# Moving projected blocks, norm steps and rows of maxima between the slots of VectorE's order

## What is computed

```python
x = x + 0.5 * ffn(layernorm(x))
x = x + attn(layernorm(x))
x = x + 0.5 * ffn(layernorm(x))
```

## Time and profile before

| | us |
|---|---|
| median of 3 runs | 2292.26 |
| lowest and highest | 2292.16, 2292.42 |
| the profiled execution's own time | 2292.54 |
| its span in the trace | 2290.7 |

### The profile page before, as it was taken

One profiled execution on the slowest core, in us unless ns is written; L12 is line 12 of the kernel. 1 busy time (PEld: TensorE's weight loads), 2 busy tenths in 40 slices (PEclk: granted clock), 3 DMA queues, 4 the chain that ended last, 5 costly groups with the idle time before them and its releaser, 6 DMA issues.

```text
span 2290.7 us, 47462 instructions
## 1 busy us (share of the span) xinstructions
PE 2220.2 (97%) x18960; PEld 1480.6 (65%) x18960; DVE 1578.8 (69%) x3138; ACT 1204.1 (53%) x1933; POOL 1064.0 (46%) x864
## 2 busy tenths in 40 slices
PE   2999999999999999999999999999999999999998
PEld 2888875555565565565555555555555655688887
DVE  7766589887777877777877876777777753454543
ACT  4433331566656666566566566666656666533332
POOL 1866653443443443443434434333433434465655
PEclk9999999999999999999999999999999999999999
DMA  5211121111111110110211111010110110011110
GB/s 216 81 42 34 39 58 30 22 41 31 35 32 40 34 51 24 33 40 22 50 42 31 32 35 32 20 42 16 26 42 11 24 36 19 26 29 36 28 39 19
DMA packets 157957, 88.26 MB, mean 39 GB/s; under 512 B 103588, under 2 KB 149924, under 8 KB 156968
## 3 DMA queue, kind: packets, MB, share of 16 engines
q1 hardware_dynamic: 157592, 85.19, 14.0%
q10 hardware_dynamic: 144, 0.03, 0.0%
HBM read 62.87 MB, written 11.80 MB: 33 GB/s over the span
## 4 chain that ended last, share of the span: by engine, by line
PE 90%; DVE 7%; issue 1%; POOL 1%; DMA 0%; ACT 0%; SPq 0%; POOLq 0%; DVEq 0%; ACTq 0%
PE PS L1193 42%; PE PS L1211 21%; PE PS L1223 11%; PE PS L1256 11%; DVE arena L968 2%; PE PS L1235 1%; PE PS L1175 1%; PE PS L1297 1%; PE PS L1283 1%; DVE XN L848 1%; DVE arena L945 1%; DVE turned L931 0%; DVE arena L930 0%; DVE parts L1044 0%; DVE arena L953 0%
## 5 line engine op out<-in xcount | busy, mean ns | idle before, releaser
L1193 PE MATMUL PS<-XT,WGU 128*128 128x256 f16 x9216 | 1115.1, 273 | 37.1 <-DVE WGU L814 20.8
L1193 PEld LDWEIGHTS PS<-XT,WGU 128*128 128x128 f16 x9216 | 876.7, 98 | 264.5 <-issue 135.4
L600 POOL TENSOR_TENSOR arena<-arena 128x512 f16<-128x512 f32 x384 | 451.1, 1175 | 1116.0 <-ACT arena L679 1115.9
L968 DVE TENSOR_REDUCE arena<-PS 128x1 f32<-128x512 f32 x1024 | 657.6, 684 | 327.4 <-PE PS L1223 325.0
L702 ACT ACTIVATE arena<-PS,fac 128x512 f32<-128x512 f32 x1024 | 647.2, 684 | 242.3 <-PE PS L1235 241.1
L672 ACT ACTIVATE arena<-PS,fac 128x512 f32<-128x512 f32 x384 | 263.9, 687 | 753.3 <-PE PS L1193 753.3
L1211 PE MATMUL PS<-WD,arena 128*128 128x256 f16 x4608 | 568.1, 273 | 7.1 <-DVE X L960 4.7
L1211 PEld LDWEIGHTS PS<-WD,arena 128*128 128x128 f16 x4608 | 431.1, 98 | 151.9 <-issue 93.6
L595 POOL TENSOR_TENSOR arena<-arena 128x512 f32<-128x512 f32 x384 | 501.2, 1305 | 46.0 <-DVE arena L953 37.5
L945 DVE SCALAR_TENSOR_TENSOR arena<-arena,PS 128x512 f32<-128x512 f32 x384 | 261.1, 680 | 263.3 <-ACT arena L672 262.4
L1223 PE MATMUL PS<-arena 48*128 48x512 f16 x1024 | 312.5, 382 | 3.3 <-DVE arena L968 2.4
(11 more groups left out here) (116 smaller groups left out, 725.9 us busy)
## 6 DMA issues: line engine op xcount, KB each, us to landing
arena<-ce_scratch SPq DMA_DIRECT2D x256, 128.0 KB, 3.2
arena<-wgu SPq DMA_DIRECT2D x4, 1536.0 KB, 12.9
arena<-q_scratch SPq DMA_DIRECT2D x192, 32.0 KB
arena<-ktab_c SPq DMA_DIRECT2D x16, 256.0 KB, 3.9
q_scratch<-arena SPq DMA_DIRECT2D x32, 128.0 KB, 1.9
out<-X SPq DMA_DIRECT2D x8, 512.0 KB, 2.9
X<-wd SPq DMA_DIRECT2D x2, 1536.0 KB, 22.8
X<-x SPq DMA_DIRECT2D x1, 3072.0 KB, 11.6
```

The costliest lines, as they stand in the source:

```text
L600: pool.tensor_tensor(hs[1][:, d % HS, :], tw[d % 2], hs[0][:, d % HS, :], ALU.subtract).then_inc(lo_done, 1)
L968: dve.tensor_reduce(mx[:, half * REP * QT + c:half * REP * QT + c + 1], PS[:, B_MAX + half, :], AX_X, ALU.max).then_inc(max_taken, 1)
L1193: ins = pe.matmul(PS[:, b, j * HALF_G:(j + 1) * HALF_G], WGU[w][:, kt, part * CHUNKS + c + j, :], XT[r][:, k % 2, kt, half * HALF_G:(half ...
```

## The change

It changes no arithmetic and no instruction, only the places. `join_slots` gives 8, 10, 14 for k = 1 and 2 and 10, 14, 16 for k = 3 to 8 (so no block in slot 12), with `rope_sum`, `rope_high`, `rope_low` and `store_block` following their block by one to three slots. In k = 1 to 8 the norm steps of group k+1 go to s = 6, 7, 9, 11, POOL's inverse roots to 8, `rows_high` and `rows_low` to 12, and SP's `turn_group` to slot 13. In the other groups these stay. On DVE `max_rows` leaves the visit: it comes behind `product` for position 0, ahead of the third visit for position 1 or behind the event, where there is no third visit, and behind the event for position 2. The loads of units wait two slots more where they use block 2.

```diff
--- before.py
+++ after.py
@@ -110,7 +110,7 @@
 
 
 
-P_HI, P_LO, P_JOIN, T_HI, T_LO, T_LOGITS = 6, 7, 8, 15, 16, 17
+P_HI, P_LO, T_HI, T_LO, T_LOGITS = 6, 7, 15, 16, 17
 
 
 BY_PE, JOINS_BY_PE = (0, 3), (0, 1)
@@ -118,9 +118,19 @@
 KV_ROWS = K_ROWS + KV * HD
 
 
-def join_slot(g):
-
-    return P_JOIN if g in JOINS_BY_PE else P_JOIN + 2
+
+NORM_AT, ALONE_AT = ((6, 7, 9, 11), 8, 12), ((9, 10, 11, 12), 10, 13)
+
+
+def steps_of_norm(k):
+
+    return NORM_AT if 1 <= k <= GROUPS else ALONE_AT
+
+
+
+def join_slots(k):
+
+    return () if k not in range(1, GROUPS + 1) else (8, 10, 14) if k - 1 in JOINS_BY_PE else (10, 14, 16)
 
 
 def event_table():
@@ -131,8 +141,8 @@
             if k - 1 in JOINS_BY_PE:
                 at[k * PER_GROUP + P_HI].append(("p_hi", k - 1, 0))
                 at[k * PER_GROUP + P_LO].append(("p_lo", k - 1, 0))
-            for j in range(JOINS):
-                at[k * PER_GROUP + join_slot(k - 1) + 2 * j].append(("join", k - 1, j))
+            for j, s in enumerate(join_slots(k)):
+                at[k * PER_GROUP + s].append(("join", k - 1, j))
         if k + 1 < PREPS:
             for s, name in ((T_HI, "t_hi"), (T_LO, "t_lo"), (T_LOGITS, "logits")):
                 if name == "logits" or k + 1 in BY_PE:
@@ -528,7 +538,7 @@
                     spread((d + 4) // 6)
                 if s == 7 and 1 <= k <= GROUPS and k - 1 not in JOINS_BY_PE:
                     turn_join(k - 1)
-                if s == 14 and 0 <= k < PREPS - 1 and k + 1 not in BY_PE:
+                if s == (13 if 1 <= k <= GROUPS else 14) and 0 <= k < PREPS - 1 and k + 1 not in BY_PE:
                     turn_group(k + 1)
                 if s == 21 and k + 1 < PREPS:
                     write_combine(k + 1)
@@ -536,21 +546,20 @@
                 if 1 <= k <= GROUPS:
                     if s == 1:
                         tables(k - 1)
-                    blk, odd = divmod(s - join_slot(k - 1) - 3, 2)
-                    if blk in range(JOINS) and not odd:
-                        store_block(k - 1, blk)
-                        if not blk:
-                            store_values(k - 1)
+                    if s - 3 in join_slots(k):
+                        store_block(k - 1, join_slots(k).index(s - 3))
+                    if s - 3 == join_slots(k)[0]:
+                        store_values(k - 1)
                 if d == FIRST - 2:
                     load(0)
                     load(1)
-                if d == FIRST:
+                if d == FIRST + 2:
                     load(2)
                 if d == FIRST + 2:
                     for u in range(2):
                         load_values(u)
                 for u in range(UNITS):
-                    if u >= QKV and d == max(SLOT_OF[FILLS * (u - QKV) + FILLS] + 1, 2 * PER_GROUP * (u // KV + 1) + 18):
+                    if u >= QKV and d == max(SLOT_OF[FILLS * (u - QKV) + FILLS] + 1, 2 * PER_GROUP * (u // KV + 1) + 18 + u % KV // 2 * 2):
                         load(u)
                     if u >= 2 and d == max(SLOT_OF[quad_visit(STEPS * (u - 1) - 1)] + 1, FIRST + 3):
                         load_values(u)
@@ -620,9 +629,8 @@
                 k, s = divmod(d, PER_GROUP)
                 if 0 <= d < SLOTS:
                     low(d)
-                blk, odd = divmod(s - join_slot(k - 1) - 2, 2)
-                if 1 <= k <= GROUPS and blk in range(JOINS) and not odd:
-                    rope_low(k - 1, blk)
+                if s - 2 in join_slots(k):
+                    rope_low(k - 1, join_slots(k).index(s - 2))
                 if d + 1 < SLOTS:
                     weigh(d + 1)
                 if 1 <= k <= GROUPS:
@@ -631,9 +639,9 @@
                     if s == 6:
                         rows_low(norm_of_join(k - 1))
                 if 0 <= k < PREPS - 1:
-                    if s == 10:
+                    if s == steps_of_norm(k)[1]:
                         inverse_roots(norm_of_group(k + 1))
-                    if s == 13:
+                    if s == steps_of_norm(k)[2]:
                         rows_low(norm_of_group(k + 1))
                 if d >= 0:
                     for name, n, j in EVENTS[d]:
@@ -764,11 +772,10 @@
                 if 1 <= k <= GROUPS:
                     if s == 6:
                         rows_high(norm_of_join(k - 1))
-                    blk, odd = divmod(s - join_slot(k - 1) - 2, 2)
-                    if blk in range(JOINS) and not odd:
-                        rope_high(k - 1, blk)
+                    if s - 2 in join_slots(k):
+                        rope_high(k - 1, join_slots(k).index(s - 2))
                 if 0 <= k < PREPS - 1:
-                    if s == 13:
+                    if s == steps_of_norm(k)[2]:
                         rows_high(norm_of_group(k + 1))
                     if s == T_LOGITS + 1:
                         exponentials(k + 1)
@@ -985,8 +992,13 @@
                 f = v + AHEAD
                 if f < VISITS:
                     maximum(f)
-                    if f % FILLS == FILLS - 1:
-                        max_rows(f // FILLS)
+
+
+            def unit_ends(v):
+
+                f = v + AHEAD
+                if f < VISITS and f % FILLS == FILLS - 1:
+                    max_rows(f // FILLS)
 
             def normalise(hv, bank):
 
@@ -1093,9 +1105,10 @@
                 if d + 1 < SLOTS:
                     gated(d + 1)
                     product(d + 1)
-                blk, odd = divmod(s - join_slot(k - 1) - 1, 2)
-                if 1 <= k <= GROUPS and blk in range(JOINS) and not odd:
-                    rope_sum(k - 1, blk)
+                if (d, 0) in VISIT:
+                    unit_ends(VISIT[d, 0])
+                if s - 1 in join_slots(k):
+                    rope_sum(k - 1, join_slots(k).index(s - 1))
                 if d == -1 or d == 0:
                     split_piece(1, d + 1)
                 if d in D_LOW_AT:
@@ -1113,14 +1126,15 @@
                 if len(EVENTS[d]) > 1:
                     event(d, 1)
                 if (d, 2) in VISIT:
+                    unit_ends(VISIT[d, 1])
                     visit(VISIT[d, 2])
                 if 1 <= k <= GROUPS and 2 <= s < 6:
                     if s == 2:
                         dve.wait_ge(x_done, 2 * k)
                     norm(norm_of_join(k - 1), k - 1, s - 2)
                 if 0 <= k < PREPS - 1:
-                    if 9 <= s < 13:
-                        norm_of(k + 1, s - 9)
+                    if s in steps_of_norm(k)[0]:
+                        norm_of(k + 1, steps_of_norm(k)[0].index(s))
                     if s == T_LOGITS + 1:
                         route(k + 1, 1)
                         route(k + 1, 2)
@@ -1132,6 +1146,10 @@
                         route(k + 1, 6)
                 if EVENTS[d]:
                     event(d, 0)
+                if (d, 2) in VISIT:
+                    unit_ends(VISIT[d, 2])
+                elif (d, 1) in VISIT:
+                    unit_ends(VISIT[d, 1])
 
 
         @block.tensor
```

## The result

| us | before | after |
|---|---|---|
| median (5 runs each, same chip) | 2292.42 | 2347.73 |
| lowest and highest | 2292.16, 2295.41 | 2343.96, 2348.87 |
| span of the profiled execution | 2290.7 | 2345.9 |
| mean granted clock | 0.999 | 0.988 |

The change makes the kernel slower: the ratio of the times is 1.0232, with a 95% interval of [1.0221, 1.0243]. That is +55 us where +29 was forecast, on the side forecast and outside the range. A span of before and one of after differ by 55.2 us, so the profiled executions can be read against each other. Counted by kind, PE is idle for 105.0 us of its span where it was idle for 70.5 (+34.5), and its instructions, the same as before, are busy for 2240.9 us where it was 2220.2 (+20.7).

The account below looks back on a forecast made before the run. The chain of waits was taken to run on PE for 90% of the span. The terms 30.7 + 9.8 + 0.7 + 1.5 - 13.5 = +29.2 us on 2292.54 us gave a forecast of 2321 us, range 2306 to 2340.

Parts of the forecast that it names:

- The first wait: PE's logits in slot 17 of k = 3 to 8 wait for the columns that SP's transposes bring: 30.7 us.
- E: End of the third block's slot, slot 16 in k = 3 to 8; columns forecast at E + 11.6.
- The gains: Waits removed: dense sum in k = 1 and 2, slots 11 to 13 of k = 3 to 8, maxima; 13.5 us.
- The maxima: Rows of maxima behind the event shorten PE's waits for the outputs' sums: 1.5 us, at most 3.2.
- The second wait: PE waits for exponentials around slots 18 and 19, the spread being late behind the transposes: 9.8 us, bounds 0 and 18.
- 0.7 for k = 1: Waits for columns and late spread in k = 1: 0.7 us, bounds 0 and 4.
- 1.5 for the clock: Half-rate clock after the waits for the columns, mostly hidden by the second wait: 1.5 us, up to 9.
- Its own sign of failure: The prediction is wrong if the logits do not wait, or PE's idle time grows elsewhere by over 15 us.
- The chain: Stores, spread, POOL's `weigh`, ACT's high parts, exponentials: spread at E + 18.5, first exponential from about E + 21.2.
- DVE's routing: In slot 18 it also waits for ACT; if late too, the second wait reaches its bound of 18 us.
- The second: Rival: each wait also costs the clock (+9 us) and lateness spreads (16 us, not 9.8); 2338 us, chance 0.16.
- The first: Rival: the first wait alone, the spread's lateness vanishing, nearly all the gain coming; 2309 us, chance 0.17.
- The third and fourth: Rivals: the columns stay hidden (2279 us, chance 0.04); the change does less than it says (2290 to 2295 us, chance 0.03).

Follow-up runs that it names:

- e8: The kernel before with only the third block of k = 3 to 8 moved to slot 16, its rope steps and store following; 2334.41 us, ratio 1.0175.
- e2: The changed kernel with `turn_group` called in slot 16 for k = 3 to 8, else 14, behind the stores and the spread; 2326.65 us, ratio 1.0144.
- e6: The changed kernel with the blocks of k = 3 to 8 back in slots 10, 12, 14 and `turn_group` in slot 14; 2286.22 us, ratio 0.9962.
- e7: e6 with the rows of maxima back inside the visit; 2285.49 us, ratio 0.9963.
- e10: The changed kernel with the spread of slot 14 moved to slot 13, ahead of the transposes, stores left behind them; 2324.82 us, ratio 1.0136.
- e3: The changed kernel with 12 to 22 extra matmuls, results overwritten, ahead of the logits of k = 3 to 8; 2349.21 us, ratio 1.0251.
- e1: The changed kernel with blocks back in slots 8, 10, 12 (k = 1, 2) and 10, 12, 14 (k = 3 to 8); 2295.79 us, ratio 1.0009.
- e11: e2 with the same 12 to 22 overwritten matmuls ahead of the logits as e3; 2317.59 us, ratio 1.0104.

## Why the prediction was right in part, and where it failed

**The first wait: right.** 30.7 us forecast, 32.7 measured in slot 17 (33.0 in e8, where nothing else is changed). The transposes started 0.2 us after E, the columns came at E + 11.7, and calling them elsewhere (e2) changes nothing.

**The gains: right in place, less in sum.** k = 1 and 2: 4.5 forecast, 5.5 measured. k = 3 to 8, slots 11 to 14: 7.5 forecast, 6.3 measured. The idle time of slots 11 to 13 fell to 4.3 us and not to the 2 that the prediction named as a sign. The maxima: 1.5 forecast, nothing shown by e6 against e7, and slot 7 of k = 4, where they now stand, holds a new 2.7 us (below). Slots 0 to 10 together lost 2.1 us. The gain is thus some 10 us, forecast 13.5.

**The second wait with its clock: the step that failed.** "Sum 9.8 us" for the spread behind the transposes, 0.7 for k = 1 and 1.5 for the clock made 12 us; measured are 27.8 in slots 18 to 21 and 4.3 in k = 1, together 32. The mechanism was right (e10: the spread alone is worth 23 us). By kind, the forecast had 27.7 us more idle time and 1.5 us for the clock; measured are 34.5 us of idle time and 20.7 us of slower matmuls. Its own sign of failure, PE's idle time growing by more than 15 us elsewhere than at the logits, did not show (3 us): what it missed was for the most part no idle time. Three things were missing in the size:

- The chain was timed too short. In k = 3 the spread came at E + 20.5 instead of 18.5. Six stores took 4.75 us of issues (494.73 to 499.48) and not 3.4: the values' four alone took 3.48, where before they took 2.22 and in the other five groups they still do. On ACT 0.39 us of the routing (`L673`) stood ahead of the exponentials. Their start, forecast for E + 21.2, is at E + 22.0 to E + 23.2 in the six groups, 8.1 us later in sum. This is read from the traces and was not tried by itself.
- The second wait and what follows from it bring falls of the clock of their own, in k = 3, 4 and 5 (in k = 4 around a wait of 2.2 us for DVE's late outputs' sum, `L1020`). Taking it away returned 8.0 us of slower matmuls in e2, and 11.9 in e10, on top of 8.7 us of idle time in each. The forecast let the second wait absorb the first one's slow stretch, which e3 bears out, and charged nothing for what comes behind the second (509.93 in the windows above). The Trainium skill (page "TensorE: Matmul & The Clock Gate", section "Part 1: The HAM clock gate") calls the half rate the default, the state of an idle engine; the trace agrees: in all six groups the granted clock falls to 0.50 during the wait for the columns (3.2 to 6.2 us long) or within 0.3 us of its end.
- DVE's routing. The prediction held it for a bound of 18 us and not for the case. In k = 1 it is about half of what PE waits for. Timeline of k = 1, slots 18 to 20:

```profile
221.63 3.08 SPq L423 DMA_DIRECT2D arena<-ce_scratch  x4
221.71 0.75 PE L1179 MATMUL PS<-WG,XT 128*128 128x32 f16 x24
...
227.54 1.26 POOL L604 TENSOR_TENSOR arena<-arena 128x512 f32<-128x512 f32 x1 [5.51 <-DMA arena<-ce_scratch]
...
229.79 0.28 DVE L889 TENSOR_REDUCE r<-pr 128x4 f32<-128x128 f32 x1 [3.85 <-ACT pr L673]
...
230.75 1.49 PE L1229 MATMUL PS<-WD,arena 128*128 128x256 f16 x12 [1.73 <-POOL arena L609]
...
232.77 2.79 PE L1211 MATMUL PS<-XT,WGU 128*128 128x256 f16 x24 [0.53 <-DVE arena L952]
...
238.44 1.81 PE L1211 MATMUL PS<-XT,WGU 128*128 128x256 f16 x15 [1.56 <-DVE arena L952]
```

The logits don't wait, as forecast. But the spread comes late. PE's `down` waits 1.7 us for the parts made from it. ACT's exponential of the routing (L673) stands behind the high part, DVE waits 3.85 us for it, and then its routing runs ahead of `gated` and `product`, for which PE waits 0.5 and 1.6 us. It is 4.3 us in all by the count, where 0.7 was forecast.

For k = 3 to 8 the forecast 9.8, the 8.1 of the chain and the 8.0 of the clock make 25.9 of the 27.8 us; the rest is not placed. The forecast was furthest off in k = 4 and 5, whose slots 18 to 21 are 5.7 and 7.1 us longer, where it had 0.5 and 3.3.

**The rivals.** The second (clock and lateness spread, 2338 us) named the lateness that spreads, and was 10 us short; but e3 gives nothing back for its other term, 9 us for the clock behind the first wait. The first fell: the spread's lateness did not vanish in the wait ahead of it. The third and fourth fell by the six waits. The sum now, from after less before: 32.7 + 27.8 + 4.3 - 5.5 - 6.3 + 2.1 and under 0.5 us elsewhere, 55 us.

## What to carry to other kernels

A step that waits on an ordered queue is released by the latest of its conditions. Calling it earlier doesn't start it earlier; it only puts everything called after it behind that condition, so follow each of those to its user: here the four DMAs of the spread, in each of seven groups, cost 23 us together, and in e1 the earlier call cost 9, through one store. When a wait is priced, add what comes behind it: its slow stretch costs nothing where the next wait hides it (e3) and 9 us where none follows (e11), the next wait can bring one of its own, and a delay that passes through SP, POOL and ACT also delays what else stands behind it in their lists, as DVE's routing in k = 1.

## What the runs showed of the hardware

Small DVE operations stretch beside POOL. The four operations of `max_rows` take 0.9 us from start to end where they run alone (0.19, 0.18, 0.19, 0.24 at 476.30 in k = 3). DVE and POOL of the changed kernel in slot 7 of k = 4:

```profile
584.81 0.64 DVE L983 TENSOR_TENSOR arena<-arena 128x32 f32<-128x32 f32 x1
585.49 1.18 DVE L984 TENSOR_SCALAR arena<-arena 128x32 f16<-128x32 f32 x1
586.70 2.07 DVE L985 SCALAR_TENSOR_TENSOR arena<-arena 128x32 f16<-128x32 f32 x1
588.80 0.25 DVE L989 STREAM_TRANSPOSE arena<-arena 128x64 f16<-128x64 f16 x1
...
585.36 1.27 POOL L604 TENSOR_TENSOR arena<-arena 128x512 f32<-128x512 f32 x1
586.58 2.14 POOL L586 TENSOR_TENSOR XS<-XN,XS 128x1024 f16<-128x1024 f32 x1
```

`L984` ends at 586.67, POOL's `L604` at 586.63; `L985` ends at 588.77, POOL's `L586` at 588.72. Each ends only when POOL's instruction is done, and the four take 4.1 us. The same is so for `L984` in all seven places where it is long: it ends within 0.1 us of POOL's. PE's scores then wait 1.54 us for the maxima (`L975`) queued behind. In the old place, inside a visit, 14 of the 16 took 0.9 to 1.0 us; in the new places 7 of 16 take 2.1 us or more, up to 4.2 (the text put on record for e7 counts 13 and 8). What that cost PE, e6 against e7 can't tell. The Trainium skill (page "SBUF — State Buffer", section "SBUF: two separate sides") describes this: DVE and GpSimd share a pair of ports under a lock held for a whole instruction. By it a DVE operation with two inputs on chip is held, which `L985` fits; `L984` has one input, and would be held only in a two-port mode, which no view here shows.

Waits much shorter than those of the logits can bring a slow stretch too. In e1, PE's wait of 2.1 us that ends at 484.45 was followed by 3.4 us at half the clock:

```profile
482.93:486.34 3.41, 1.70 (x13) 1.00 0.53 88
486.34:489.75 3.41, 3.41 (x17) 0.50 0.66 184
```

In the changed kernel 1.3 us of idle time were enough in slot 19 of k = 3 (the windows from 506.52 above).
